# An attention and mixture-of-experts layer on 8 cores: the next window's layer norms cut into pieces between projections, and break points in TensorE's background work

## The chip, the cores and the metric

The kernel runs on the 8 cores of one Trainium2 chip. Each core takes 2048 of the 16384 tokens and works alone. The metric is the device time of the slowest core, in microseconds (us). Before the change it is 2968.38 us, the median of 3 runs (2964.4 to 2970.36).

The engines of a core are named as the profile names them: PE is TensorE (matmuls; PEld its weight loads), DVE is VectorE, ACT is ScalarE, POOL is GpSimd, SP is SyncE, which here only issues DMAs.

## The reference

What is computed, cut to what matters (LN is a layer norm without scale and shift):

```python
def layer(x):                                   # x: (2, 8192, 1024)
    h = LN(x)
    Q, K, V = h @ W_q + b_q, h @ W_k + b_k, h @ W_v + b_v
    Q, K, V = [(a).reshape(n, 16, l, 64) for a in (Q / 32, K / 32, V)]
    A = softmax(einsum('neax,nebx->neab', Q, K), axis=2)    # over a
    out = diagonal(A, axis1=2, axis2=3)[..., None] * V
    x = x + out.reshape(n, l, 1024) @ W_o + b_o
    f = LN(x)
    e = argmax(f @ Wr.T + br)                   # one of 8 experts for each token
    return x + W2[e] @ relu(W1[e] @ f + b1[e]) + b2[e]
```

The reshape makes 512 consecutive tokens of the program's input one head: within such a window of 512 tokens each token gives 16 queries and 16 keys of 64 elements, and only the diagonal of the softmax is used, so the kernel needs the sum of exp(score) for each of 8192 rows of a window and nothing else of the scores.

## The kernel before

**Windows.** A core has four windows (w = 0 to 3) of 512 tokens. For each it must compute the scores of 8192 by 8192, take their exponential and sum them. That is done in 64 rows of score tiles (r), each in five score groups of 3, 3, 4, 3, 3 (or 3, 3, 3, 4, 3) tiles of 128x512. PE writes a group into one half of PSUM (line 407), ACT takes exp over it with a running sum (line 520), and the two halves alternate: PE may write group n only when ACT is done with group n-2. So there are 320 score groups in a window and 1280 in all.

**Background work.** Everything else of the attention is cut into units by Python generators on PE's side and put between the score groups. After each group PE's budget `spare` grows by 1.5 or 2.5 units (at most 1.0 is carried over), and the loop takes units from the generator `fill` until the budget is used up. A unit is about one matmul of 128x512. What the units are:

- `proj` (line 253): 8 matmuls for 128 channels of Q, K or V over the window's 512 tokens. DVE then evacuates the tile with a bias (lines 591, 605 and 615).
- `swap_k` (line 264) and `diag` (line 272): after a tile of keys, the halves of its partitions swapped, and the diagonal scores, which serve as the exponent's offset. DVE makes what they read (605, 608) and takes what they give (596, 598).
- `xlt` (line 239): transposes of a normed tile of 128 tokens, which DVE copies to `XLT` (line 586).
- `tail`: when a quarter of a window (128 tokens, t = 0 to 3) has its sums, the reciprocal is turned (317), spread over the heads (326, twice), multiplied with V by DVE (645), projected with `W_o` (339), added to x (651), transposed (353), and put through the router (363, 374, 375). In between stand the pieces of the next window's Q, K, norms and of this window's V, as the table `PIECES[quarter][gap]` says: four quarters, in each four gaps in the tail.

**One bank.** During the attention all background work shares a single PSUM bank (`ONE_BANK`). A unit that takes the bank waits until DVE has evacuated the bank's last content, and DVE takes its instructions strictly in the order in which they are written. PE also takes its own in order, so while a background unit waits, the next score group waits behind it.

**Norms.** `norm(w, tc)` on DVE (line 578) makes one tile of 128 tokens: two `bn_stats`, one `bn_aggr`, ten steps on one column each (mean, variance, and three Newton steps for the inverse root), then the normed tile into one of two `XN` buffers. Two of the four norms of the next window stand together, `("n", 0), ("n", 1)`, in the first gap of quarter 0; the other two are in the first gap of quarter 1. For window 1 the first two follow the eight V tiles of window 0 directly.

**After the attention** the last quarter's tail runs alone, and then eight experts, in which PE runs matmuls of 320 columns nearly without a pause.

Of the kernel before, what the change touches and what calls it, by code (L numbers as in the profile page):

```python
# [9 lines left out]
F32 = mybir.dt.float32  # L10
# [6 lines left out]
P = 128  # L17
# [35 lines left out]


PIECES = (
# [11 lines left out]
def build_nc():  # L67
# [26 lines left out]
    with ExitStack() as st:  # L94
# [29 lines left out]
        NWU = S("NWU", [P, 1], F32); NWY = S("NWY", [P, 1], F32)  # L124
        NMN = S("NMN", [P, 1], F32)
        LG = S("LG", [P, 8], F32); LW = S("LW", [P, 8], F32)
        RMX = S("RMX", [P, 1], F32); RM2 = S("RM2", [P, 1], F32)
# [86 lines left out]
        def _(e):  # L214
# [16 lines left out]
            def pause(n):  # L231
                for _ in range(n):
                    yield 0

            def xlt(w, tc):
                b = bank()
                e.wait_ge(vXN, 4 * w + tc + 1)
                for c in range(DC):
                    mm = e.transpose(bf(b)[:, c * P:(c + 1) * P],
                                     XN[:, tc % 2, c * P:(c + 1) * P], IDB[:])  # L240
                    if c % 2 == 1 and c < DC - 1:
                        yield 1
                mm.then_inc(pM, 1)
                MARK["xlt", w, tc] = kM
                yield 1

            def proj(w, g, mc):
                if w == 0 and mc == 0:
                    e.wait_ge(sW[g], 16)
                b = bank()  # L250
                e.wait_ge(vM, MARK["xlt", w, 3])
                for kc in range(DC):
                    mm = e.matmul(PS[:, b, :], WR[:, g, kc, mc * P:(mc + 1) * P], XLT[:, kc, :],  # L253
                                  start=(kc == 0), stop=(kc == DC - 1))
                    if kc < DC - 1:
                        yield 1
                mm.then_inc(pM, 1)
                MARK["qkv"[g], w, mc] = kM
                yield 1

            def swap_k(w, c):
                b = bank()
                e.wait_ge(vM, MARK["k", w, c])
                e.matmul(PS[:, b, :], SWAP[:], KB[w % 2][:, c, :], start=True, stop=True).then_inc(pM, 1)
                MARK["s", w, c] = kM
                yield 1

            def diag(w, c):
                b = bank()
                e.wait_ge(vPR, DC * w + c + 1)  # L270
# [41 lines left out]
            def tail(w, t, pw, q):  # L312
# [7 lines left out]
                yield from pieces(pw, q, 0)  # L320
                for h in range(2):
                    b = bank()
                    if h == 0:
# [8 lines left out]
                if w + t == 0:  # L332
                    e.wait_ge(sW[3], 16)
                for hh in range(2):
                    b = bank()
                    if hh == 0:
# [9 lines left out]
                yield from pause(2)  # L346
                for hh in range(2):
                    b = bank()
                    if hh == 0:
# [36 lines left out]
            for w in range(NR):  # L386
# [7 lines left out]
                for r in range(64):  # L394
# [6 lines left out]
                    for size in SLOTS[r % 2]:  # L401
# [11 lines left out]
                        n += 1  # L413
                        spare = min(spare + SPARE[size], SPARE[size] + 1.0)
                        while spare > 0 and r >= hold:
                            cost = next(fill, 0)
                            if cost < 0:
                                hold = -cost
                            elif cost == 0:
                                break  # L420
                            else:
                                spare -= cost
                for _ in fill:
                    pass
# [123 lines left out]
        def _(e):  # L548
# [9 lines left out]
            def step(op):  # L558
# [4 lines left out]
                e.wait_ge(vS, nS)  # L563

            def stats(xt):

                for i in range(2):
                    step(e.bn_stats(BN6[:, i, :], xt[:, i * 512:(i + 1) * 512]))  # L568
                step(e.bn_aggr(MV[:], BN6[:].rearrange("p a b -> p (a b)")))
                step(e.tensor_scalar(NMN[:], MV[:, 0:1], -1.0, None, ALU.mult))  # L570
# [6 lines left out]

            def norm(w, tc):
                e.wait_ge(sXA[tc], 16 * (w + 1))
                stats(XA[:, tc, :])  # L580
                e.tensor_scalar(XN[:, tc % 2, :], XA[:, tc, :], NMN[:], NWY[:],
                                ALU.add, ALU.mult).then_inc(vXN, 1)
# [35 lines left out]
            def pieces(w, q, gap):  # L618
                for kind, i in PIECES[q][gap] if w < NR else ():
                    if kind == "v":  # L620
                        value(i)
                    elif w + 1 < NR:
                        if kind == "n":
                            norm(w + 1, i)
                        elif kind == "x":
# [70 lines left out]
            step(e.tensor_scalar(BKS[:], BKS[:], SCALE, None, ALU.mult))  # L696
            norm(0, 0)
            norm(0, 1)
            xlt(0)
            norm(0, 2)  # L700
            xlt(1)
            norm(0, 3)
            xlt(2)
# [11 lines left out]
            step(e.tensor_scalar(CN1[:], CN0[:], float(FIRST + 1), None, ALU.add))  # L715
            for c in range(DC):
                value(c)
            norm(1, 0)
            norm(1, 1)
            for w in range(NR):  # L720
# [306 lines left out]
```

## Time and profile before

| | |
|---|---|
| median of the runs | 2968.38 us |
| profiled execution | 2967.23 us |
| its span, first to last instruction, slowest core | 2965.5 us |
| spans of the eight cores | 2955.9 to 2965.5 us |
| PE busy | 2255.3 us, 76% |
| ACT busy | 2164.3 us, 73% |
| DVE busy | 539.5 us, 18% |
| chain that ended last | PE 41%, ACT 40%, issue 12%, DVE 5% |

The shares are means over two stages with different limits. In the attention ACT's exponentials fill most of the time; in the experts it is PE. "Granted clock" is the share of TensorE's full 2.4 GHz that the chip let through; 0.50 is its lower level of 1.2 GHz.

### The profile page before, as it was taken

The numbers are of one execution on the slowest core, as the hardware profiler recorded it, in microseconds if no ns is written. First come the engines' busy times: TensorE is split into PE (matmuls) and PEld (weight loads), VectorE is DVE, ScalarE is ACT, GpSimd is POOL, SyncE is SP. The second block draws the span as 40 slices with busy tenths as digits, with TensorE's granted clock in tenths as the row PEclk, the third lists the DMA queues.
The fourth block names the chain that finished last, engine by engine and source line by source line (L and its number), as shares of the span: only waits on it lengthen the run. The fifth ranks groups of instructions, "written<-read, shape, count | busy, mean of one in ns | idle before, by whom it ended". The sixth has DMA issues, their size and how long they took to land.

```text
span 2965.5 us, 31530 instructions; the slowest of 8 cores (2955.9 to 2965.5 us)
## 1 busy us (share of the span) xinstructions
PE 2255.3 (76%) x10592; PEld 840.3 (28%) x10592; DVE 539.5 (18%) x1309; ACT 2164.3 (73%) x2721; POOL 144.2 (5%) x201
## 2 busy tenths in 40 slices
PE   3876777867776878676767777776676599999997
PEld 1221111211121212111112121111111277777775
DVE  3113111121220112212111111110110212222221
ACT  0897999898989998898999889999999211111110
POOL 0000000000000000001000000000000001111100
PEclk9686675657675656675776657655555699999998
DMA  9999999999999999993000000030000278878773
GB/s 188 135 108 113 118 118 123 116 119 115 117 115 121 124 117 116 115 116 45 18 8 11 1 18 7 11 124 0 11 8 4 75 245 257 256 251 257 251 243 83
DMA packets 38163, 324.55 MB, mean 109 GB/s; under 512 B 8784, under 2 KB 9680, under 8 KB 25712
## 3 DMA queue, kind: packets, MB, share of 16 engines
q0 software_dynamic: 16224, 157.39, 45.7%
q1 hardware_dynamic: 21776, 165.05, 16.6%
q8 instruction: 95, 1.56, 0.2%
q14 instruction: 68, 0.56, 0.1%
HBM read 443.70 MB, written 159.73 MB: 203 GB/s over the span
## 4 chain that ended last, share of the span: by engine, by line
PE 41%; ACT 40%; issue 12%; DVE 5%; DMA 1%; DVEq 0%; SPq 0%; POOL 0%; ACTq 0%; POOLq 0%
ACT EA L520 20%; ACT EB L520 20%; PE PS L407 11%; PE PS L479 9%; PE PS L491 9%; PE PS L253 5%; PE PS L272 1%; PE PS L363 1%; PE PS L339 1%; DVE BN L568 1%; DVE AR L605 1%; PE PS L453 1%; DMA GM<-c_gm 1%; DVE AR L596 1%; PE PS L353 1%
## 5 line engine op out<-in xcount | busy, mean ns | idle before, releaser
L407 PE MATMUL PS<-AR 64*128 64x512 bf16 x4096 | 1124.4, 538 | 492.5 <-ACT EA L520 274.1
L520 ACT ACTIVATE EA<-PS,NEGD 128x1536 bf16<-128x1536 f32 (+1 forms) x640 | 1120.1, 1750 | 86.0 <-PE PS L407 83.8
L520 ACT ACTIVATE EB<-PS,NEGD 128x1536 bf16<-128x1536 f32 x640 | 1010.9, 1580 | 75.7 <-PE PS L407 75.0
L407 PEld LDWEIGHTS PS<-AR 64*128 64x128 bf16 x4096 | 172.9, 100 | 1221.2 <-issue 1218.1
L253 PE MATMUL PS<-XLT,WR 128*128 128x512 bf16 x768 | 307.6, 486 | 14.3 <-DVE VB L615 7.1
L532 ACT ACTIVATE AR<-PS,B1C 128x320 bf16<-128x320 f32 x128 | 67.5, 527 | 274.7 <-PE PS L479 274.7
L491 PE MATMUL PS<-AR,WR 128*128 128x320 bf16 x1664 | 229.9, 299 | 0.0
L479 PE MATMUL PS<-AR,WR 128*128 128x320 bf16 x1600 | 224.1, 301 | 1.0 <-DVE AR L742 1.0
L538 ACT ACTIVATE XR<-PS,B2C 128x320 f32<-128x320 f32 x32 | 16.9, 527 | 270.7 <-PE PS L491 270.7
L491 PEld LDWEIGHTS PS<-AR,WR 128*128 128x128 bf16 x1664 | 162.1, 98 | 62.0
L479 PEld LDWEIGHTS PS<-AR,WR 128*128 128x128 bf16 x1600 | 157.4, 98 | 62.5 <-issue 1.3
L520 ACT ACTIVATION_READ_ACCUMULATOR EB<-PS,NEGD 128x1 f32 x640 | 156.9, 245 | 0.0
L520 ACT ACTIVATION_READ_ACCUMULATOR EA<-PS,NEGD 128x1 f32 x640 | 156.3, 244 | 0.0
L253 PEld LDWEIGHTS PS<-XLT,WR 128*128 128x128 bf16 x768 | 61.2, 105 | 287.8 <-issue 279.0
L767 DVE TENSOR_SCALAR AR<-PS,B1C 128x320 bf16<-128x320 f32 x128 | 70.3, 549 | 196.2 <-PE PS L479 187.1
L635 DVE TENSOR_REDUCE ZS<-ZC 128x16 f32<-128x80 f32 x16 | 3.8, 235 | 547.4 <-ACT EB L520 547.4
L339 PE MATMUL PS<-WR,SA 128*128 128x512 bf16 x256 | 95.7, 459 | 1.7 <-DVE SA L645 1.1
L605 DVE TENSOR_SCALAR AR<-PS,BKS 128x512 bf16<-128x512 f32 x32 | 24.0, 751 | 243.1 <-PE PS L253 243.1
L363 PEld LDWEIGHTS PS<-WRT,X1T 128*128 128x128 f32 x256 | 53.4, 290 | 50.4 <-issue 50.4
L615 DVE TENSOR_SCALAR VB<-PS,BV 128x512 bf16<-128x512 f32 x32 | 24.0, 751 | 226.0 <-PE PS L253 226.0
L272 PE MATMUL PS<-GM,PROD 128*128 128x2 f32 x256 | 47.2, 306 | 23.4 <-DVE AR L596 22.5
L923 POOL DMA_DIRECT2D w1b<-w1t x64 | 31.5, 492 | 666.5 <-DMA w1b<-w1t 604.9
(93 smaller groups left out, 1093.8 us busy)
## 6 DMA issues: line engine op xcount, KB each, us to landing
w1b<-w1t POOLq DMA_DIRECT2D x64, 1024.0 KB, 19.4
w2b<-w2t POOLq DMA_DIRECT2D x64, 1024.0 KB
WR<-w2b SPq DMA_DIRECT2D x26, 2048.0 KB
WR<-w1b SPq DMA_DIRECT2D x25, 2048.0 KB
XA<-w1b SPq DMA_DIRECT2D x7, 2048.0 KB
XA<-w2b SPq DMA_DIRECT2D x6, 2048.0 KB
XA<-x SPq DMA_DIRECT2D x16, 512.0 KB, 53.4
XR<-x SPq DMA_DIRECT2D x16, 512.0 KB, 44.7
```

Source lines behind the costliest of these rows:

```text
L253: mm = e.matmul(PS[:, b, :], WR[:, g, kc, mc * P:(mc + 1) * P], XLT[:, kc, :], start=(kc == 0), stop=(kc == DC - 1))
L272: mm = e.matmul(PS[:, b, 2 * t0:2 * t0 + 2], PROD[:, c % 2, t0 * P:(t0 + 1) * P], GM2[:], start=True, stop=True)
L339: mm = e.matmul(PS[:, b, :], SA[:, kc, :], WR[:, 3, kc, hh * 512:(hh + 1) * 512], start=(kc == 0), stop=(kc == DC - 1))
L363: mm = e.matmul(PS[:, b, 0:8], X1T[:, c, :], WRT[:, c, :], start=(c == 0), stop=(c == DC - 1))
L407: mm = e.matmul(PS[:, (n % 2) * 4 + i, :], kb[w % 2][hp:hp + 64, gb // 2, t0 * P:(t0 + 1) * P], QB[w % 2][hp:hp + 64, ga // 2, :], start=T ...
L479: mm = e.matmul(PS[:, b, 0:cols], w1[:, kc, (k % 8) * P:(k % 8 + 1) * P], XGF[:, eg % 2, kc, 0:cols], start=(kc == 0), stop=(kc == DC - 1))
L491: mm = e.matmul(PS[:, b, 0:cols], w2[:, j, (dc % 2) * P:(dc % 2 + 1) * P], HB[:, j, 0:cols], start=(j == 0), stop=(j == NF - 1))
L520: e.activation(EO[n % 2][:, 0:size * 512], PS[:, b0:b0 + size, :].rearrange("p a b -> p (a b)"), AF.Exp, bias=NEGD[:, w % 2, t0, gb:gb + 1 ...
L532: e.activation(HB[:, k, 0:cols], PS[:, k % 4, 0:cols], AF.Relu, bias=B1C[:, ei * NF + k:ei * NF + k + 1]).then_inc(aCH, 1)
L605: e.tensor_scalar(KB[w % 2][:, c, :], PS[:, b, :], SCALE, BKS[:, c:c + 1], ALU.mult, ALU.add).then_inc(vM, 1)
L767: e.tensor_scalar(HB[:, k, 0:cols], PS[:, k % 4, 0:cols], B1C[:, ei * NF + k:ei * NF + k + 1], 0.0, ALU.add, ALU.max).then_inc(vCH, 1)
L923: e.dma_start(out=w1b[ei][i * 128:(i + 1) * 128, :], in_=w1t[ei][i * 128:(i + 1) * 128, :]).then_inc(sC1, 16)
```

## The change

Two things are changed, and a third goes with the first.

1. **Norms in pieces.** `norm` is split in three. `tile_moments` makes mean and variance of one tile (two `bn_stats`, one `bn_aggr`). `tile_scales` makes offset and inverse root for all four tiles at once, in 13 steps of four columns. `tile_norm` writes one normed tile. In the table `PIECES` these are kinds "s", "c" and "a". They have no work on PE. Those of quarter 0 each stand in front of the evacuation of a V projection, the last two between the transposes of quarter 1. The table's entry for the first gap of quarter 0 is now empty.
2. **Break points.** Each unit that takes the bank first yields `None` (`breath`), except the router's. The loop stops there, if it has already taken a unit behind this score group, and goes on behind the next one.
3. At the program's start and for window 1 the norms are written in the same new form.

```diff
 PIECES = (
-    ((("n", 0), ("n", 1)), (("v", 0), ("v", 1), ("v", 2)),
-     (("v", 3), ("v", 4), ("v", 5)), (("v", 6), ("v", 7))),
-    ((("x", 0), ("n", 2), ("x", 1), ("n", 3)), (("x", 2), ("x", 3)),
+    ((), (("s", 0), ("v", 0), ("s", 1), ("v", 1), ("s", 2), ("v", 2)),
+     (("s", 3), ("v", 3), ("c", 0), ("v", 4), ("a", 0), ("v", 5)), (("a", 1), ("v", 6), ("v", 7))),
+    ((("x", 0), ("a", 2), ("x", 1), ("a", 3)), (("x", 2), ("x", 3)),
...
+            def breath():
+
+                yield None
+
             def xlt(w, tc):
+                yield from breath()
                 b = bank()
...
             def proj(w, g, mc):
+                yield from breath()
...
             def swap_k(w, c):
+                yield from breath()
                 b = bank()
...
             def diag(w, c):
+                yield from breath()
                 b = bank()
...
                         spare = min(spare + SPARE[size], SPARE[size] + 1.0)
+                        begun = False
                         while spare > 0 and r >= hold:
                             cost = next(fill, 0)
-                            if cost < 0:
+                            if cost is None:
+                                if begun:
+                                    break
+                            elif cost < 0:
                                 hold = -cost
                             elif cost == 0:
                                 break
                             else:
                                 spare -= cost
+                                begun = True
...
+            def tile_moments(w, tc):
                 e.wait_ge(sXA[tc], 16 * (w + 1))
-                stats(XA[:, tc, :])
-                e.tensor_scalar(XN[:, tc % 2, :], XA[:, tc, :], NMN[:], NWY[:],
+                moments(XA[:, tc, :], MVX[:, tc, :])
+
+            def tile_scales():
+
+                step(e.tensor_scalar(NMX[:], MVX[:, :, 0], -1.0, None, ALU.mult))
+                step(e.tensor_scalar(NXH[:], MVX[:, :, 1], 0.5, 0.5 * EPS, ALU.mult, ALU.add))
+                step(e.tensor_scalar(NXI[:], NXH[:].bitcast(I32), 1, None, ALU.logical_shift_right))
+                step(e.tensor_scalar(NWX[:].bitcast(I32), NXI[:], -1.0, MAGIC, ALU.mult, ALU.add))
+                for _ in range(3):
+                    step(e.tensor_tensor(NXU[:], NWX[:], NWX[:], ALU.mult))
+                    step(e.tensor_tensor(NXU[:], NXU[:], NXH[:], ALU.mult))
+                    step(e.scalar_tensor_tensor(NWX[:], NXU[:], 1.5, NWX[:], ALU.subtract, ALU.mult))
+
+            def tile_norm(tc):
+                e.tensor_scalar(XN[:, tc % 2, :], XA[:, tc, :], NMX[:, tc:tc + 1], NWX[:, tc:tc + 1],
                                 ALU.add, ALU.mult).then_inc(vXN, 1)
...
-            norm(0, 0)
-            norm(0, 1)
+            for tc in range(4):
+                tile_moments(0, tc)
+            tile_scales()
+            tile_norm(0)
+            tile_norm(1)
             xlt(0)
-            norm(0, 2)
+            tile_norm(2)
             xlt(1)
-            norm(0, 3)
+            tile_norm(3)
             xlt(2)
             xlt(3)
...
             for c in range(DC):
+                if c < 4:
+                    tile_moments(1, c)
+                elif c == 4:
+                    tile_scales()
+                elif c < 7:
+                    tile_norm(c - 5)
                 value(c)
-            norm(1, 0)
-            norm(1, 1)
```

On DVE, at the start of window 1, before the change: the end of the second of two norms of `XA`, then the two products with V (`SA`), then three V tiles (`VB`).

```order
L575 SCALAR_TENSOR_TENSOR NWU<-NWY,NWH 128x1
L576 SCALAR_TENSOR_TENSOR NWY<-NWU,NWY 128x1
L581 TENSOR_SCALAR XN<-XA,NMN,NWY 128x1024
L645 TENSOR_TENSOR SA<-PS,VB 128x512 x2
L615 TENSOR_SCALAR VB<-PS,BV 128x512 x3
L651 TENSOR_TENSOR XR<-PS,XR 128x512 x2
```

The same place on DVE after the change, from the copy of the turned sums (`WRS`) on.

```order
L680 COPY WRS<-PS 16x128
L684 TENSOR_TENSOR SA<-PS,VB 128x512 x2
L586 BN_STATS BN<-XA 128x6 x2
L587 BN_AGGR MVX<-BN 128x2
L650 TENSOR_SCALAR VB<-PS,BV 128x512
L586 BN_STATS BN<-XA 128x6 x2
L587 BN_AGGR MVX<-BN 128x2
L650 TENSOR_SCALAR VB<-PS,BV 128x512
```

Between `WRS` and `SA` nothing is left; the moments of a tile stand ahead of each V tile.

On PE, in quarter 3 of window 0, before: score groups (L407) with the units between them. `KB` and `KS` are parts of `AR`; L264 is `swap_k`, L272 `diag`, L326 the spreading over heads.

```order
L407 MATMUL PS<-AR 128x512 x3
L253 MATMUL PS<-XLT,WR 128x512
L407 MATMUL PS<-AR 128x512 x3
L264 MATMUL PS<-AR,SWAP 128x512
L272 MATMUL PS<-GM,PROD 128x2 x4
L407 MATMUL PS<-AR 128x512 x10
L326 MATMUL PS<-WRS,GMB 128x128 x8
```

The same place after the change (L421 are the score groups).

```order
L421 MATMUL PS<-AR 128x512 x3
L262 MATMUL PS<-XLT,WR 128x512
L421 MATMUL PS<-AR 128x512 x3
L274 MATMUL PS<-AR,SWAP 128x512
L421 MATMUL PS<-AR 128x512 x3
L283 MATMUL PS<-GM,PROD 128x2 x4
L421 MATMUL PS<-AR 128x512 x7
L338 MATMUL PS<-WRS,GMB 128x128 x4
L421 MATMUL PS<-AR 128x512 x3
L338 MATMUL PS<-WRS,GMB 128x128 x4
```

A score group now stands between `swap_k` and `diag`, and one between the two halves of the spreading.

## Rows read from the trace of the kernel before

**Rows 1.** Busy time by stretch: attention, and all behind it

```profile
core 0: us, PE busy (x) PEld busy (x) DVE busy (x) ACT busy (x) POOL busy (x), PEclk, DMA share, GB/s
73.00:2314.00 2241.00, 1626.29 (x5943) 387.11 (x5943) 365.48 (x978) 2079.08 (x2561) 77.46 (x143) 0.64 0.60 75
2314.00:2965.00 651.00, 604.13 (x4531) 441.25 (x4531) 146.16 (x257) 84.33 (x160) 62.73 (x50) 0.96 0.68 218
```

**Rows 2.** Waits of ACT in the attention: total us, times, longest

```profile
ACT EA L520 <- PE PS L407: 83.8, 70, 8.9
ACT EB L520 <- PE PS L407: 75.0, 82, 12.0
```

**Rows 3.** ACT timeline (start, us): first group, score row 46 and next, last group

```profile
73.38 1.54 ACT L520 ACTIVATE EA<-PS,NEGD 128x1536 bf16<-128x1536 f32 x1
...
490.84 1.57 ACT L520 ACTIVATE EA<-PS,NEGD 128x1536 bf16<-128x1536 f32 x1
...
498.84 1.60 ACT L520 ACTIVATE EB<-PS,NEGD 128x1536 bf16<-128x1536 f32 x1
...
2312.04 1.67 ACT L520 ACTIVATE EB<-PS,NEGD 128x1536 bf16<-128x1536 f32 x1
```

**Rows 4.** ACT timeline: the groups behind norms, with the idle before them

```profile
243.79 1.54 ACT L520 ACTIVATE EB<-PS,NEGD 128x1536 bf16<-128x1536 f32 x1 [12.04 <-PE PS L407]
...
260.44 1.54 ACT L520 ACTIVATE EA<-PS,NEGD 128x1536 bf16<-128x1536 f32 x1 [5.03 <-PE PS L407]
...
674.68 1.97 ACT L520 ACTIVATE EA<-PS,NEGD 128x2048 bf16<-128x2048 f32 x1 [8.91 <-PE PS L407]
...
820.49 1.97 ACT L520 ACTIVATE EA<-PS,NEGD 128x2048 bf16<-128x2048 f32 x1 [6.81 <-PE PS L407]
```

**Rows 5.** Waits of PE in the attention, those on DVE: total us, times, longest

```profile
PE PS L326 <- DVE SA L645: 42.8, 15, 8.6
PE PS L272 <- DVE AR L596: 22.5, 24, 1.2
PE PS L264 <- DVE AR L605: 16.5, 20, 1.2
PE PS L317 <- DVE DGT L637: 12.7, 1, 12.7
```

**Rows 6.** Start of the program, timeline of POOL, DVE and PE

```profile
14.88 0.93 POOL L914 DMA_DIRECT2D WR<-wk  x1 [12.04 <-DMA XA<-x]
...
24.67 1.49 DVE L568 BATCH_NORM_STATS2 BN<-XA 128x6 f32<-128x512 f32 x2 [0.17 <-DVE BKS L696]
26.27 0.21 DVE L569 BATCH_NORM_AGGREGATE MV<-BN 128x2 f32<-128x12 f32 x1
...
29.43 0.81 DVE L581 TENSOR_SCALAR XN<-XA,NMN,NWY 128x1024 bf16<-128x1024 f32 x1
...
47.28 0.81 DVE L581 TENSOR_SCALAR XN<-XA,NMN,NWY 128x1024 bf16<-128x1024 f32 x1
...
50.19 17.45 PE L253 MATMUL PS<-XLT,WR 128*128 128x512 bf16 x72 [0.94 <-DVE XLT L586]
```

**Rows 7.** The DMA issue of the K weights, us to landing last

```profile
WR<-wk POOLq DMA_DIRECT2D x1, 2048.0 KB, 26.3
```

**Rows 8.** PE and ACT, joined units (window 0, quarter 3)

```profile
523.47 0.38 PE L264 MATMUL PS<-AR,SWAP 128*128 128x512 bf16 x1 [0.46 <-DVE AR L605]
...
524.89 1.84 PE L272 MATMUL PS<-GM,PROD 128*128 128x2 f32 x8 [1.05 <-DVE AR L596]
...
527.79 1.54 ACT L520 ACTIVATE EB<-PS,NEGD 128x1536 bf16<-128x1536 f32 x1 [2.48 <-PE PS L407]
```

**Rows 9.** PE and ACT, the same units with a score group between them

```profile
591.70 0.38 PE L264 MATMUL PS<-AR,SWAP 128*128 128x512 bf16 x1 [0.45 <-DVE AR L605]
...
593.12 1.02 PE L272 MATMUL PS<-GM,PROD 128*128 128x2 f32 x8 [0.35 <-DVE AR L596]
...
594.96 1.55 ACT L520 ACTIVATE EB<-PS,NEGD 128x1536 bf16<-128x1536 f32 x1
```

**Rows 10.** PE at its lower clock: units and score groups in turn

```profile
290.71 1.01 PE L253 MATMUL PS<-XLT,WR 128*128 128x512 bf16 x2
291.65 1.03 PE L407 MATMUL PS<-AR 64*128 64x512 bf16 x3
292.62 1.04 PE L253 MATMUL PS<-XLT,WR 128*128 128x512 bf16 x2
```

More of the change, by code:

```diff
@@ L125, in build_nc @@
         NMN = S("NMN", [P, 1], F32)
+        MVX = S("MVX", [P, 4, 2], F32); NMX = S("NMX", [P, 4], F32); NWX = S("NWX", [P, 4], F32)
+        NXH = S("NXH", [P, 4], F32); NXI = S("NXI", [P, 4], I32); NXU = S("NXU", [P, 4], F32)
         LG = S("LG", [P, 8], F32); LW = S("LW", [P, 8], F32)
@@ L321, in tail @@
                 for h in range(2):
+                    yield from breath()
                     b = bank()
@@ L334, in tail @@
                 for hh in range(2):
+                    yield from breath()
                     b = bank()
@@ L347, in tail @@
                 for hh in range(2):
+                    yield from breath()
                     b = bank()
@@ L563, in step, with moments, stats @@
                 e.wait_ge(vS, nS)
-            def stats(xt):
+            def moments(xt, mv):
                 for i in range(2):
                     step(e.bn_stats(BN6[:, i, :], xt[:, i * 512:(i + 1) * 512]))
-                step(e.bn_aggr(MV[:], BN6[:].rearrange("p a b -> p (a b)")))
+                step(e.bn_aggr(mv, BN6[:].rearrange("p a b -> p (a b)")))
+            def stats(xt):
+                moments(xt, MV[:])
                 step(e.tensor_scalar(NMN[:], MV[:, 0:1], -1.0, None, ALU.mult))
@@ L576, in stats @@
                     step(e.scalar_tensor_tensor(NWY[:], NWU[:], 1.5, NWY[:], ALU.subtract, ALU.mult))
-            def norm(w, tc):
+            def tile_moments(w, tc):
                 e.wait_ge(sXA[tc], 16 * (w + 1))
-                stats(XA[:, tc, :])
-                e.tensor_scalar(XN[:, tc % 2, :], XA[:, tc, :], NMN[:], NWY[:],
+                moments(XA[:, tc, :], MVX[:, tc, :])
[10 more added lines that the diff above has]
+                e.tensor_scalar(XN[:, tc % 2, :], XA[:, tc, :], NMX[:, tc:tc + 1], NWX[:, tc:tc + 1],
                                 ALU.add, ALU.mult).then_inc(vXN, 1)
@@ L622, in pieces @@
                     elif w + 1 < NR:
-                        if kind == "n":
-                            norm(w + 1, i)
+                        if kind == "s":
+                            tile_moments(w + 1, i)
+                        elif kind == "c":
+                            tile_scales()
+                        elif kind == "a":
+                            tile_norm(i)
                         elif kind == "x":
@@ L716, in _ @@
             for c in range(DC):
+                if c < 4:
+                    tile_moments(1, c)
+                elif c == 4:
+                    tile_scales()
+                elif c < 7:
+                    tile_norm(c - 5)
                 value(c)
-            norm(1, 0)
-            norm(1, 1)
             for w in range(NR):
```

## The prediction

> **What bounds the kernel now.** I read the busy time by stretch first. It splits the profiled execution at 2314 us: before it lies the attention, with ACT busy for 2079 of 2241 us; behind it the experts, with PE busy for 604 of 651 us at a granted clock of 0.96 [rows 1]. The change writes nothing behind 2314 us, so I take those 651 us as fixed, and ask what the attention's 2241 us and the 73 us ahead of it lose.
>
> In the attention the reader should look for how far ACT is from running back to back. One row of five score groups takes 498.84 - 490.84 = 8.00 us where nothing disturbs it; 256 of them make 2048 us. The attention lasts from 73.38 us to the end of the last group, 2312.04 + 1.52, which is 2240 us [rows 3]. So 192 us are lost. The waits of ACT show the same: 83.8 + 75.0 = 158.8 us in 152 waits, all on PE's score groups [rows 2]. (The view gives less than 192 because it leaves out the shortest gaps and because about 0.1 to 0.25 us of reading the accumulator, which otherwise overlaps, is exposed at each.) That is all that any change of the background work can win.
>
> Next, why PE was late. Its waits on DVE in this stretch are 42.8 + 22.5 + 16.5 + 12.7 = 94.5 us in the four largest rows, and about 117 us with a dozen small ones [rows 5]. PE runs in order, so a unit waiting for DVE holds the next score group back. The other 75 us or so of the 192 are PE's own work: bursts of units that are too long for one group's period at the lower clock. Two units and the next score group start 1.91 us apart (290.71 to 292.62) [rows 10], against the 1.52 us that ACT needs for three tiles.
>
> The change touches both kinds of DVE wait: the norms, and the short waits for the one bank.
>
> **The start.** Today four norms of some 5.5 to 6 us stand in a chain, each with its ten single steps, from 24.67 us to the first projection at 50.19 us [rows 6]. From the first norm: the two `bn_stats` with the aggregate take 26.27 - 24.67 + 0.31 = 1.91 us; from there to 29.43 us is 2.85 us for ten steps, 0.285 us a step. New chain: four moments 4 x 1.91 = 7.6 us; 13 steps 3.7 us (four columns instead of one; I give them the same price, since these times are hardly those of elements); then until the last norm starts, three norms of 0.73 us and two copies of 0.7 us, 3.6 us. That puts the last norm at 39.6 us, and from there to the first projection is 50.19 - 47.28 = 2.9 us as now: 42.5 us instead of 50.2. I take 7 us of the 7.7. The new form needs all four input tiles before the first norm; they are there, since POOL saw them by 14.88 us. Behind it are eight Q projections without a wait, 14 us at the 17.45 us for 72 matmuls, so K weights are wanted at 56 us; they were issued at 14.88 us and landed 26.3 us later, at 41 us [rows 6, 7]. Bounds: 4 us if the steps of four columns are twice as dear, 8 us else. **-7 us.**
>
> **The norms.** ACT stands 12.04 and 5.03 us behind the two pairs of norms in window 0, 8.91 and 6.81 us in window 1 [rows 4]; window 2 repeats window 1's with 8.92 and 7.00. The sum is 48.7 us; window 3 has no successor. What comes in their place: four moments of 1.9 us, one block of 13 steps of 3.7 us, and norms of 0.8 us, each in front of a V evacuation. What hides them is the V projection itself. It has 8 units and is spread over five or six score groups of 1.52 us, so DVE has about 7.5 us from one V tile to the next, and is busy for only 365 of 2241 us [rows 1]. The longest piece plus the evacuation, 3.7 + 0.75 us, fits. If that cover were gone the piece would hold back one evacuation, and PE would wait for the rest of it: 15 us of pieces a window, which is again the old loss. In quarter 1 a norm of 0.8 us remains between two transposes; that too falls under the score group which now follows. In window 0, the turning of the sums follows the last V unit with no break and waits for that evacuation and four short DVE steps, about 1 us beyond what is hidden. Bounds: 40 us (a fifth stays) to 50 us. **-48 us.**
>
> **The breaks.** Of the 117 us of PE's waits on DVE, about 49 are the norms', the 12.7 and the five long ones under the 42.8 [rows 5]. The other 68 are evacuations awaited by a unit that follows another one in the same gap. In the joined form swap and diagonal wait 0.46 and 1.05 us and ACT then idles 2.48 us [rows 8]. With a score group between them, which the old order happens to give at one place in each of windows 0 to 2, PE still waits 0.45 and 0.35 us, but those waits fall in time that PE has, and ACT's group at 594.96 us starts without idle [rows 9]. By the order of instructions there are 54 gaps of the joined kind before the change and 3 after it; groups with more than one bank unit behind them nearly vanish, while the number of score groups with any unit rises from 739 to 787.
>
> Not all 68 us come home. The diagonal's matmuls take 1.84 us at the lower clock against 1.02 at the higher [rows 8, 9]; with the next score group's 0.97 us that is 2.8 us in a period of 1.52, so even a lone diagonal costs about 0.9 us in perhaps 16 of its 30 places, 14 us. The break also leaves budget over, and up to 1.0 unit of it is spent at once later: openings with three projection matmuls rise from 30 to 46, and nine with four appear. A quarter of the saving could go that way, but the joined gaps that it replaces carried the same matmuls, so I book only 2 us. 68 - 14 - 2 = 52. Bounds: 20 us (only the longest joined gaps gain) to 68 us. **-52 us.** No unit is pushed out of its window: the last unit of windows 0 to 2 stands behind score group 304 of 320, before it was 303.
>
> **The sum.** 7 + 48 + 52 = 107 us. Against the profiled execution's own 2967.2 us (its span 2965.5 and 1.7 around it): 2860.2 us. The median of the runs shown lies 1.2 us above that execution, so 2861 us; the attention would lose 92 us to waiting instead of 192.
>
> **The clock.** Over the attention the granted clock is 0.64 on average, a mixture of the two levels 0.50 and 1.00 [rows 1]. The Trainium skill says against this change ("TensorE: Matmul & The Clock Gate", section "A second HAM failure mode: psum-queue depth-cycling") that short idle times between groups of matmuls make the clock swing between its two levels, and that what is lost is the time at the lower one; breaks make more and shorter pauses. By that rule the second rival below would come out. In this trace both levels occur beside such pauses already, so it bears the rule out only in part.
>
> **The rivals.**
>
> *Breaks only move the waits.* The bank is still one, and the budget left over comes back as longer bursts. Then the breaks win nothing and the norms and the start all: 2968.4 - 7 - 48 = 2913 us. For it: openings of three matmuls rise by half. Against it: the separated pair in rows 9 runs without idle.
>
> *The lower clock throughout, slower than before.* Place: the attention. If PE stayed at 0.50 in all of it, each gap would have its price at that level. The new order has 318 score groups with two units behind them, 1.91 - 1.52 = 0.39 us each, 124 us; 172 with three or more, at 0.47 a unit 0.83 us or so, 142 us; 297 with one unit give back 0.07 each (21 us), and 94 stretches without units give back one lead of about 0.42 (39 us). 124 + 142 - 21 - 39 = 206 us lost, more than the 192 of today, and where the leads are not won back 245. With the start's 7 us: 2968.4 - 7 + 14 = 2975, up to 3014; I take 2985 us. It decides from where the attention loses more than 199 us. Against it: DVE waits vanish, so PE stands still less.
>
> *Higher clock.* A mean of 0.64 from levels 0.50 and 1.00 means 72% of the attention at the lower level [rows 1]. If without the long waits it were 62%, a seventh of the 92 us of bursts (13 us) would go, and most of the lone diagonals' 14 us, which arise at the lower level alone: 2861 - 26 = 2835 us.
>
> *The pieces don't hide.* V evacuations held up by moments, half of the norms' loss comes back: 2885 us.
>
> **How the numbers follow.** Main case 2861 us: 0.68, own range 2843 to 2885. Breaks move the waits, 2913: 0.12. Lower clock, slower: 0.03. Higher clock, 2835: 0.10. Pieces not hidden, 2885: 0.07. The range of 8 in 10 reaches from 2833 to 2902 us: the lower end takes in most of the higher-clock case and the bounds 8, 50 and 68; the upper one reaches part-way to the first rival. What a measurement of this kernel can tell from no change is about 0.2%, 6 us. All cases but the lower clock are faster by more than that, and part of that case lands within it: faster 0.96, same 0.01, slower 0.03.
>
> **What would show it.** In the profile after: first exp at about 66 us; no ACT idle above 3 us in the attention; 256 rows in about 2140 us; PE's waits on DVE for the spreading over heads under 8 us instead of 42.8; `swap` and `diag` still waiting a few tenths each without ACT idle at the higher clock; the stretch behind the attention still 651 us. I am wrong in the breaks if ACT's waits stay above 110 us, in the norms if a gap of 5 us or more remains, and in the clock if the attention's mean is off 0.64 by 0.05 or more.

## The result, and the profile after

The kernel after takes 2844.61 us, the median of 4 runs (2841.02 to 2919.44), against 2967.62 us (2964.4 to 2970.36) for the kernel before on the same chip. The ratio is 0.9581, with a 95% interval of 0.9566 to 0.9596: 123 us or 4.2% faster. Forecast were 2861 us, within 2833 to 2902. The run of 2919.44 us is one in which part of the chip was disturbed; the ratios and the ranges of runs below leave such runs out and the medians don't, so where they disagree the ratio is to be read.

The profiled execution's span is 2839.3 us on its slowest core, 126.2 us less than before. First the busy time by stretch on core 0, which answers [rows 1]; the columns are the same.

```profile
67.00:2188.00 2121.00, 1569.21 (x5869) 378.06 (x5940) 350.28 (x896) 2072.73 (x2560) 78.17 (x143) 0.67 0.63 80
2188.00:2839.00 651.00, 603.76 (x4530) 441.44 (x4531) 146.18 (x257) 84.81 (x162) 62.74 (x50) 0.96 0.65 218
```

The stretch behind the attention is 651 us, as it was. The attention has gone from 2241 us to 2121 us with nearly the same ACT work, and its mean granted clock from 0.64 to 0.67 (0.65 to 0.67 as the mean of the eight cores). So all of the gain lies in two places, the start and ACT's idle time in the attention. This is the start on core 0 (start us, busy us, engine, line, operation), which answers [rows 6, 3]:

```profile
25.29 1.49 DVE L586 BATCH_NORM_STATS2 BN<-XA 128x6 f32<-128x512 f32 x2 [0.17 <-DVE BKS L735]
...
33.13 0.17 DVE L606 TENSOR_SCALAR NMX<-MVX 128x4 f32<-128x4 f32 x1
...
37.07 1.53 DVE L616 TENSOR_SCALAR XN<-XA,NMX,NWX 128x1024 bf16<-128x1024 f32 x2
...
43.99 2.29 PE L262 MATMUL PS<-XLT,WR 128*128 128x512 bf16 x5 [0.95 <-DVE XLT L621]
...
67.14 1.54 ACT L539 ACTIVATE EA<-PS,NEGD 128x1536 bf16<-128x1536 f32 x1
```

The first projection starts at 43.99 us instead of 50.19, and the first exponential at 67.14 instead of 73.38: 6.2 us less, although the chain of norms starts 0.62 us later than it did. The chain itself is therefore 6.8 us shorter.

The waits of ACT and of PE in the attention, on core 0 (who waits for whom: us in total, times, longest), which answer [rows 2, 5]:

```profile
ACT EB L539 <- PE PS L421: 24.4, 57, 2.1
ACT EA L539 <- PE PS L421: 20.5, 41, 2.5
```

```profile
PE PS L283 <- DVE AR L631: 4.4, 9, 1.1
PE PS L274 <- DVE AR L640: 2.4, 6, 0.6
PE PS L262 <- DVE VB L650: 2.3, 4, 0.7
PE PS L328 <- DVE DGT L676: 1.8, 1, 1.8
```

ACT waits 44.9 us instead of 158.8, and no wait is longer than 2.5 us where the longest was 12.04. PE's waits on DVE add up to 12.6 us instead of about 117. The spreading over heads (L338 now, L326 before), which carried the largest of them with 42.8 us, has no row at all.

For the comparisons below I use one measure of ACT's loss: the distance from the start of an exponential to the start of the next, less 1.515 us for three tiles or 1.94 us for four (4 x 1.515 + 1.94 = 8.00 us, the undisturbed row of [rows 3]). Summed over the attention it gives 192 us before and 73 us after on core 0, and 189.0 and 70.2 us as means of the eight cores. Sorted by what stands between the score groups, the means of the eight cores are:

| us lost by ACT | before | after |
|---|---|---|
| gaps with `swap_k` or `diag` | 56.4 | 11.6 |
| gaps with the spreading or the turning (the norms stood there) | 59.4 | 1.7 |
| other gaps with several users of the bank | 15.4 | 0 |
| gaps with one unit or with bursts of matmuls | 54.9 | 54.1 |

(Gaps without any unit hold the missing 3 us.) What is left after the change is nearly all PE's own work, and nearly all of it is lost at the lower clock: of the 70.2 us, 65 fall in places where the granted clock was 0.50 from the one exponential to the next, and 1.7 where it was 1.00. Before, it was 161 and 9.6 us of 189.0.

At the place of the old gap of 8.91 us [rows 4], window 1 on core 0 now reads:

```profile
616.04 1.68 ACT L539 ACTIVATE EB<-PS,NEGD 128x1536 bf16<-128x1536 f32 x1
616.43 1.04 PE L421 MATMUL PS<-AR 64*128 64x512 bf16 x4
617.40 0.60 PE L338 MATMUL PS<-WRS,GMB 16*128 16x128 bf16 x4
617.57 2.10 ACT L539 ACTIVATE EA<-PS,NEGD 128x2048 bf16<-128x2048 f32 x1
618.72 1.48 DVE L586 BATCH_NORM_STATS2 BN<-XA 128x6 f32<-128x512 f32 x2
619.43 1.06 PE L262 MATMUL PS<-XLT,WR 128*128 128x512 bf16 x2 [0.47 <-issue]
619.53 1.66 ACT L539 ACTIVATE EB<-PS,NEGD 128x1536 bf16<-128x1536 f32 x1
```

The two halves of the spreading (L338) have a score group between them, and ACT runs back to back. The batch statistics begin at 618.72 us, where nothing on PE waits for DVE. (The 0.47 us ahead of the projection's row is a matmul that is missing from the records; its weight load stands in the trace at 619.02 us.)

And the swap and the diagonal at the place where [rows 8] had them joined:

```profile
487.92 0.39 PE L274 MATMUL PS<-AR,SWAP 128*128 128x512 bf16 x1
488.66 1.55 ACT L539 ACTIVATE EA<-PS,NEGD 128x1536 bf16<-128x1536 f32 x1
488.92 0.59 PE L421 MATMUL PS<-AR 64*128 64x512 bf16 x3 [0.61 <-ACT EB L539]
489.44 1.05 PE L283 MATMUL PS<-GM,PROD 128*128 128x2 f32 x8
490.17 1.55 ACT L539 ACTIVATE EB<-PS,NEGD 128x1536 bf16<-128x1536 f32 x1
491.69 1.99 ACT L539 ACTIVATE EA<-PS,NEGD 128x2048 bf16<-128x2048 f32 x1
```

ACT's idle time of 2.48 us has gone entirely. Two things differ here, not one: the diagonal also took 1.05 us, the price of the higher clock, where it took 1.84 us before.

### The profile page after: what moved, and what is told of

Its sections match the earlier page's. It is cut to its first block, busy times and chain, and to the rows that moved or that the text cites. A ratio compares the mean times of both kernels' runs of the same rounds, so it can differ in the third digit from the quotient of the medians.

```text
span 2839.3 us, 31237 instructions; the slowest of 8 cores (2830.4 to 2839.3 us)
## 1 busy us (share of the span) xinstructions
PE 2197.8 (77%) x10515; PEld 831.5 (29%) x10592; DVE 519.6 (18%) x1201; ACT 2158.7 (76%) x2721; POOL 144.9 (5%) x201
## 4 chain that ended last, share of the span: by engine, by line
ACT 47%; PE 37%; issue 13%; DVE 1%; DMA 1%; SPq 0%; POOL 0%; DVEq 0%; ACTq 0%; POOLq 0%
ACT EA L539 24%; ACT EB L539 23%; PE PS L498 10%; PE PS L510 10%; PE PS L421 9%; PE PS L262 4%; PE PS L377 1%; PE PS L283 1%; PE PS L472 1%; DMA GM<-c_gm 1%; PE PS L352 0%; PE PS L458 0%; DVE BN L586 0%; DMA out_t<-VB,PAD 0%; PE PS L367 0%
## 5 line engine op out<-in xcount | busy, mean ns | idle before, releaser
L421 PE MATMUL PS<-AR 64*128 64x512 bf16 x4096 | 1107.3, 526 | 518.1 <-ACT EA L539 291.2
L421 PEld LDWEIGHTS PS<-AR 64*128 64x128 bf16 x4096 | 171.7, 99 | 1213.9 <-issue 1211.7
L262 PE MATMUL PS<-XLT,WR 128*128 128x512 bf16 x707 | 282.2, 482 | 18.8 <-issue 11.0
L352 PE MATMUL PS<-WR,SA 128*128 128x512 bf16 x240 | 85.6, 435 | 4.8 <-issue 2.5
L498 PE MATMUL PS<-AR,XA 128*128 128x320 bf16 x448 | 62.8, 299 | 0.0
L973 POOL DMA_DIRECT2D w2b<-w2t x64 | 31.5, 492 | 598.4 <-DMA w2b<-w2t 598.4
```

Source lines behind the costliest of these rows:

```text
L352: mm = e.matmul(PS[:, b, :], SA[:, kc, :], WR[:, 3, kc, hh * 512:(hh + 1) * 512], start=(kc == 0), stop=(kc == DC - 1))
L421: mm = e.matmul(PS[:, (n % 2) * 4 + i, :], kb[w % 2][hp:hp + 64, gb // 2, t0 * P:(t0 + 1) * P], QB[w % 2][hp:hp + 64, ga // 2, :], start=T ...
L498: mm = e.matmul(PS[:, b, 0:cols], w1[:, kc, (k % 8) * P:(k % 8 + 1) * P], XGF[:, eg % 2, kc, 0:cols], start=(kc == 0), stop=(kc == DC - 1))
L973: e.dma_start(out=w2b[ei][i * 128:(i + 1) * 128, :], in_=w2t[ei][i * 128:(i + 1) * 128, :]).then_inc(sC2, 16)
```

## The experiments

Unless something else is said, the edit is shown against the kernel after (- is a line taken out, + one put in), and the loss is ACT's by the measure above, the mean of eight cores. Ratios are to the kernel before, with their 95% intervals.

**Norms only.** The norms' new form, with the break points silent, so that PE's order is that of before.

```diff
 def breath():
+    return
     yield None
```

> The norms in pieces (start included), no break points: TensorE's order is that of the kernel before. Theory A (the two parts add up, each removes its own waits on VectorE): the six gaps of 5 to 12 us vanish and the start gains 6 us, so 2967 - 49 - 6 = about 2912 us; ScalarE's waits in the attention stay near 110 us. Theory B (the pieces need the breaks, because without a score group between units a moment in front of a V evacuation is waited for): less than half of the 49 comes, 2935 us or more. Theory C (the breaks do nothing but move waits): 2845 to 2855 us, as the full change.

Measured: ratio 0.9857 [0.9747, 0.9967], runs 2922.8 to 2936.3 us, and a loss of 149.0 us: 40.0 less than before. The joined gaps are as they were. On core 1 PE still waits at the diagonal and the swap, as much as in [rows 5]:

```profile
PE PS L284 <- DVE AR L632: 24.2, 27, 1.2
PE PS L275 <- DVE AR L641: 15.1, 18, 1.2
PE PS L339 <- DVE SA L685: 14.2, 15, 0.9
```

The spreading (L339) has kept 15 waits of at most 0.9 us; the long ones behind norms are gone. At the norms' own places the loss fell by 41.9 us. By these waits the pieces hide; the 17.5 us that stay in these gaps are those of the spreadings and turnings themselves, which still stand joined. The six gaps behind norms alone lost 49.9 us before and lose 7.7 now, so only 42.2 us of them were the norms'. That is theory A's mechanism, but not its number: the runs lie 11 to 24 us above its 2912 us.

**Breaks only.** The old norms, at the start too, with the break points active.

```diff
-((), (("s", 0), ("v", 0), ("s", 1), ...
+((("n", 0), ("n", 1)), (("v", 0), ("v", 1), ("v", 2)), ...
-((("x", 0), ("a", 2), ("x", 1), ("a", 3)), ...
+((("x", 0), ("n", 2), ("x", 1), ("n", 3)), ...
```

> The break points alone, norms whole and in their old places, start as before; TensorE's order is that of the full change. Theory A (the parts add up): the full change gained about 125 us, of which start 6 and norms 49, so the breaks are worth 70 us: 2897 us; the six gaps of 5 to 12 us are still there. My prediction's size for the breaks, 52 us, would give 2915 us. Theory C (breaks only move waits): within 6 us of 2967 us.

Measured: ratio 0.9755 [0.9672, 0.9838], runs 2896.2 to 2909.8 us, a loss of 120.9 us: 68.1 less than before. PE's waits on DVE on core 2:

```profile
PE PS L338 <- DVE SA L686: 28.5, 5, 7.6
PE PS L328 <- DVE DGT L678: 12.7, 1, 12.7
...
PE PS L274 <- DVE AR L646: 3.6, 7, 0.6
PE PS L283 <- DVE AR L637: 3.5, 7, 1.0
```

Swap and diagonal together wait 7.1 us instead of 39.0. Of the long waits only the norms' remain, six of up to 12.7 us. So the breaks do not move the waits to another place. In bursts they do give some back: ACT loses 75.5 us less in the first three kinds of gap of the table, and 7.9 us more in gaps with one unit or bursts (62.8 against 54.9). The two parts alone give 40.0 + 68.1 = 108.1 us, and together 118.8.

**The start only.**

```diff
 # the table, norm() and window 1 as in the kernel before
 def breath():
+    return
     yield None
```

> Only the first window's norms at the program's start in the new form; all else as before. Theory A: the first exponential comes 6 to 7 us earlier and the end follows one for one, 2961 us (ratio 0.998). Rival: the start is hidden behind weights or constants that land later, 2967 us.

Measured: 2960.58 us, ratio 0.9971 [0.9943, 0.9998], about 7 us less (by the interval, just told apart from no change), with an attention that loses as much as before (187.4 us). The waits of ACT over the whole span, on the slowest core; the third is the one ahead of the first score group, and the other two are nearly those of [rows 2]:

```profile
ACT EA L540 <- PE PS L422: 83.6, 63, 9.3
ACT EB L540 <- PE PS L422: 75.6, 81, 12.4
ACT L540 <- PE PS L422: 66.0, 1, 66.0
```

The start is worth what the sum gave it.

**Breaks at swap and diagonal only.** The new norms; the other units (`xlt`, `proj`, the tail's) take the bank without a break.

```diff
 def proj(w, g, mc):
-    yield from breath()
...  # the same in xlt and at three places of tail
```

> Norms in pieces, and breaks only in front of the key swap and the diagonal; projections, transposes, head spreading and output projection follow each other without a break. In the trace before, gaps with swap and diagonal joined to something else carried about 47 of the 74 us that ScalarE idled behind joined units. Theory A1 (each joined gap pays for itself): 47 of the breaks' 70 us are kept, 2912 - 47 = 2865 us. Theory A2 (what counts is that no unit waits for the bank anywhere): well above that, 2885 us. Theory A3 (the other breaks cost more in longer bursts than they save): 2845 us or less.

Measured: ratio 0.9685 [0.958, 0.9789], median 2880.1 us, a loss of 105.2 us. The gaps with swap or diagonal fell from 55.2 us (norms only) to 17.1, while the spreading's 15.6 and the other joined gaps' 16.0 are near norms only's 17.5 and 15.1. On core 1 PE's waits on DVE are again, in the first place, those of the units that were left joined:

```profile
PE PS L335 <- DVE SA L679: 14.2, 15, 0.9
PE PS L260 <- DVE VB L645: 8.9, 9, 1.1
PE PS L362 <- DVE X1T L689: 5.7, 6, 0.9
```

Swap (L272) and diagonal (L281) wait 4.2 and 3.9 us here. The time is nearer to the 2885 us of theory A2, but only because theory A1 counted from 2912 us: norms only came out at 2926 us (the middle one of its runs), and 47 us less is 2879. So A1 holds: each kind of joined gap pays for itself, and parting one hardly touches the others.

**Moments and scales in one block.** What the pieces would cost if nothing covered them: all four moments and the scales in the first gap of quarter 0, as the norms stood.

```diff
-((), (("s", 0), ("v", 0), ("s", 1), ("v", 1), ("s", 2), ("v", 2)),
- (("s", 3), ("v", 3), ("c", 0), ("v", 4), ("a", 0), ("v", 5)), ...
+((("s", 0), ("s", 1), ("s", 2), ("s", 3), ("c", 0)), (("v", 0), ("v", 1), ("v", 2)),
+ (("v", 3), ("v", 4), ("a", 0), ("v", 5)), ...
```

> The full change, but in windows 1 and 2 the moments of all four tiles and the scales stand as one block in the first gap of quarter 0, behind the turned sums, where no projection covers them; the two norms of single tiles stay in front of V tiles. TensorE's order is that of the full change. It tests whether it is the place in front of a projection that hides the work. Theory A (only the cover counts): the block is 4 x 1.9 + 3.7 = 11.3 us; of the two old norms' 11 us in that place ScalarE idled 8.9 us, so some 9 us come back in each of two windows, 18 us, 2863 us; ScalarE shows two gaps of about 9 us. Theory B (a long wait also sends TensorE to its lower clock, and the bursts behind it cost more): 25 us or more, of which 7 or more lie outside the two gaps. Theory C (shorter work is enough, since four tiles share one set of scale steps): 5 us or less.

Measured: 2865.32 us, ratio 0.9654 [0.9639, 0.9669], 21 us slower than the kernel after, with a loss of 91.3 us. Here is DVE on core 6 in window 1, and the exponential that waited:

```profile
614.99 1.47 DVE L586 BATCH_NORM_STATS2 BN<-XA 128x6 f32<-128x512 f32 x2
...
622.80 0.17 DVE L606 TENSOR_SCALAR NMX<-MVX 128x4 f32<-128x4 f32 x1
...
626.04 0.16 DVE L613 SCALAR_TENSOR_TENSOR NWX<-NXU,NWX 128x4 f32<-128x4 f32 x1
```

```profile
628.85 1.54 ACT L539 ACTIVATE EB<-PS,NEGD 128x1536 bf16<-128x1536 f32 x1 [7.42 <-PE PS L421]
```

Four moments take 622.80 - 614.99 = 7.8 us and the 13 steps 3.4 us, against 7.6 and 3.7 in the prediction. The same work costs nothing in pieces and 7.4 us in a block. That makes 15.2 us in the two windows that have it. The other 6.0 us appeared in gaps with one unit or bursts, 3.7 of them in the first 80 groups of windows 1 and 2, behind the blocks: from score group 9 to 80 of window 1 the granted clock was 0.73 (mean of eight cores) where the kernel after has 0.78. So the result lies between theories A and B.

**Half the budget carried over.** An opening is a place where a projection begins; this removes most openings with three or four matmuls in one gap (55 before the edit, 12 with it).

```diff
-spare = min(spare + SPARE[size], SPARE[size] + 1.0)
+spare = min(spare + SPARE[size], SPARE[size] + 0.5)
```

> The full change with at most 0.5 instead of 1.0 unit of budget carried over. Openings with three or four projection matmuls fall from 55 to 12, the last unit of a window stands behind score group 307 instead of 304. In the trace after the change ScalarE idled 24 us behind those openings, of 73 us in all. Theory A (a burst costs because it is longer than one group's period and the lead; two units cost 0.39 us only where no lead is left): half of it goes, 2844 - 12 = 2832 us. Theory B (the same matmuls must be done somewhere, the idle only moves to the groups with two units): within 4 us of 2844 us.

Measured: 2840.25 us, ratio 0.9584 [0.9556, 0.9611], a loss of 69.0 us: no difference. ACT's waits (core 6) have only changed their shape, to more and shorter ones:

```profile
ACT EA L539 <- PE PS L421: 22.0, 63, 1.5
ACT EB L539 <- PE PS L421: 11.2, 35, 1.2
```

The matmuls of the long openings, spread out, cost the same elsewhere: gaps with three or four projection matmuls lose 18.3 us less, and those with two 16.7 us more.

**The diagonal in two halves, and more breaks.**

```diff
 # diag, after two of its matmuls
+if t0 == 1:
+    yield 2.5
...
-yield 2
+yield 1
 # and breath() ahead of router_sums, the router's logits and the turning
```

> The full change, with the diagonal's four matmuls cut into two pairs with a score group between them at most places, and break points also ahead of the router's units and of the turning of the sums. Theory A (the lone diagonal, 1.84 us at the lower clock, is still too long for a period; my prediction put 14 us on it, the trace after shows 6): 5 us of 11 us go, with 3 us more at the added breaks: 2844 - 8 = 2836 us. Theory B (no bank unit waits that could still be parted; longer background work only pushes bursts together): within 4 us of 2844 us.

Measured: 2847.88 us, ratio 0.9596 [0.9583, 0.9609], a loss of 74.1 us: nothing gained, possibly 4 us lost. ACT's waits on core 1:

```profile
ACT EB L544 <- PE PS L426: 27.5, 74, 0.8
ACT EA L544 <- PE PS L426: 22.0, 50, 2.4
```

The diagonal's long turn was not a cost worth removing.

**An extra score matmul.** The first matmul of a score group is issued twice where no unit preceded it, 489 times by the weight loads in the trace; the second overwrites the first with the same values.

```diff
-spare, hold = 0.0, 0
+spare, hold, begun = 0.0, 0, True
...
+if i == 0 and not begun:
+    mm = e.matmul(PS[:, (n % 2) * 4 + i, :], ...)   # once more
```

> The full change; in each score group that follows a group behind which no unit was taken (492 of them) the first tile's matmul is done twice, the second writing the same values. It adds work where TensorE is least busy, to see what the granted clock does. Theory A (the remaining 54 us of idle behind bursts come from the lower clock, and more activity raises it): the attention's granted clock goes from 0.66 to 0.75 or more, the idle falls by 10 to 25 us, 2820 to 2835 us. Theory B (the clock stays and the added 0.34 us a group fits into the period): 2844 us within 4. Theory C (the added work takes the lead that the next burst needs): 2850 us or more.

Measured: 2918.47 us, ratio 0.9833 [0.9819, 0.9846], 74 us slower than the kernel after, 0.15 us for each of the 489. The attention's row on core 7:

```profile
67.00:2187.00 2120.00, 1746.97 (x6245) 437.65 (x6243) 350.42 (x896) 2026.83 (x2469) 77.75 (x143) 0.66 0.63 80
```

By the records PE is busy for 1746.97 - 1569.21 = 178 us more in these 2120 us than in the kernel after, and the granted clock was 0.66 where that has 0.67. More work on PE did not bring it up. And a gap without background work is no free time: of the 76 us that ACT loses more (146.4 against 70.2), 63 lie in these very gaps. 453 of them were at the lower clock, where a matmul in a row of them takes 0.34 us [rows 10] and the added one cost 0.14 us; in the 24 at the higher clock it cost nothing. The other 13 us were lost elsewhere, which is what theory C spoke of: the lead that the next burst needs.

**A thinner order.** Less budget for each group, so that the units spread more evenly: first 1.25 and 2.25 with half a unit carried over, then 1.2 and 2.0. The third run is the kernel after again, for comparison on the same chip.

```diff
-SPARE = {3: 1.5, 4: 2.5}
+SPARE = {3: 1.25, 4: 2.25}      # the second: {3: 1.2, 4: 2.0}
...
+spare = min(spare + SPARE[size], SPARE[size] + 0.5)
```

> The full change with a smaller budget of background work behind each score group: 1.25 and 2.25 units instead of 1.5 and 2.5, at most 0.5 carried. The same units stand in 919 instead of 787 places, and places with more than two units fall from 172 to 83; the last unit of windows 0 to 2 stands behind group 313 of 320. Theory A (the remaining 70 us of idle are bursts longer than a period, so spreading them thinner helps): 12 to 20 us less than the full change, 2828 us. Theory B (as when only the carry was cut: the idle moves to places with two units, and the lead between bursts is what sets it): within 5 us of the full change, 2844 us. Theory C (thinner work lowers the granted clock): 2850 us or more.

> As the one before, with 1.2 and 2.0 units: 923 places with units, 51 with more than two, 327 with two. Theory A: 15 to 25 us less than the full change, 2824 us. Theory B: 2844 us within 5. Theory C: 2850 us or more, and a lower granted clock in the attention than 0.67.

> The changed kernel once more, on the same chip and in the same rounds as the two thinner orders, so that the three can be compared. All theories: 2844 us within 5.

Measured:

| | ratio, 95% | runs, us | loss, us |
|---|---|---|---|
| thin | 0.9543 [0.9511, 0.9574] | 2834.4 to 2838.5 | 63.6 |
| thinner | 0.9534 [0.9488, 0.9581] | 2832.7 to 2834.2 | 62.2 |
| after, again | 0.9581 [0.9543, 0.9619] | 2839.7 to 2850.1 | 71.2 |

The attention in the thinner order (core 1) and in the kernel after again (core 6):

```profile
67.00:2187.00 2120.00, 1656.81 (x5956) 390.34 (x5956) 353.22 (x903) 2072.82 (x2560) 77.67 (x143) 0.65 0.63 80
```

```profile
67.00:2187.00 2120.00, 1590.59 (x5939) 380.91 (x5939) 350.29 (x896) 2072.13 (x2559) 77.75 (x143) 0.67 0.63 80
```

The thinner order loses 9 us less although its clock is 0.65 and not 0.67, and PE is busy for 66 us more in it. A better clock is not what makes the difference between these orders. Gaps with one unit or bursts lose 17 us less (37.9 against 54.9), and those with swap, diagonal, spreading or turning 9 us more (22.4 against 13.7). It is the best version that was run: all its runs lie below all of the kernel after, by 13 us (0.5%) from middle to middle. The intervals of the ratios overlap, so the size of that gain is not settled. Theory A's direction is right; its 15 to 25 us are not quite reached.

## Why the prediction was right, and which term was mis-sized

**What bounds the kernel.** Right: all the gain came from ACT's idle time and the start, and the 651 us behind the attention stayed 651.

**The start, -7.** Measured -6.2 us in the profile, and about -7 us with the start alone. Right, and so was its working: 7.8 us for the moments (25.29 to 33.13) and 3.9 for the steps (to 37.07) against 7.6 and 3.7. The first projection came at 43.99 us and not at 42.5; 0.6 of these 1.5 us are the later start of the chain.

**The norms, -48.** The mechanism was right: the pieces hide behind the V projection, and uncovered they cost 7.4 us a window. Alone they gave 40.0 us, the lower bound. The 48.7 us that I read behind the norms were not all theirs: 7.7 us of those six gaps stayed with norms only, since the spreading and the turning still stood joined there, and went only with the breaks. Added to the breaks the pieces gave 120.9 - 70.2 = 50.7 us, of which 41.1 at their own places.

**The breaks, -52.** This is the term that was mis-sized. Alone the breaks gave 68.1 us, which was my bound and not my value, and the deduction of 14 us for diagonals that stand alone was the step that failed. I had priced 16 of 30 such places at the lower clock with 0.9 us. In the kernel after there are 29, and they lose 7.6 us (mean of eight cores): 12.5 of them lie wholly at the lower clock and lose 0.57 us each, the others 0.4 us in all. And 11 diagonals stood alone before already and lost 9.3 us, so nothing was to be deducted for the rest.

The term's other two numbers were off too, but against each other. I had read a joined gap's cost as PE's wait on DVE alone, 68 us (it was 71, since the norms' waits were 12.7 + 33.4 = 46 us and not 49); with the breaks alone all gaps with swap, diagonal, spreading, turning or several users of the bank lost 75.5 us less. And for budget left over I had booked 2 us, where the gaps with one unit or bursts lost 7.9 us more. Only together with the norms' pieces did these gaps lose nothing more (54.9 and 54.1). Openings of three matmuls cost 46 x 0.35 us and those of four 9 x 0.60, 21.5 us together, against 30 x 0.63 = 18.8 before, and shortening them gave nothing back.

**The sum.** It left the attention a loss of 92 us; 73 us are left on core 0. Against the 100 us of the two terms the eight cores gained 118.8: 8.0 less from the norms alone, 16.1 more from the breaks alone, and 10.7 more because the two together give more than their sum. Errors of opposite sign thus brought the forecast nearer than its terms were. The last 10.7 us are not explained. They lie in gaps with one unit or bursts: the pieces alone made these lose 3.4 us more and the breaks alone 7.9, and both together 0.8 less; in every other kind of gap the two parts add up within 1 us. The clock goes with it in part. Behind the norms' place in window 1, from group 9 to 80, it is 0.78 after, 0.74 with breaks only and 0.73 with the block, so in the new order a long wait is followed by a lower clock. But before has 0.76 there, with the long wait, and norms only 0.75, without it. Why the old order differs stays open.

**The rivals.** That the breaks only move the waits (2913 us) fell with the breaks-only run: swap and diagonal waited 7.1 us and not 39.0. That the pieces don't hide (2885 us) fell too; with the block, where they can't, the time was 2865 us. The lower clock throughout, and slower, did not come: the mean rose to 0.67. And the breaks did not make more and shorter pauses, as I had argued: in the attention of core 0 PE waited 922 times before, for 0.66 us on average, and 898 times after, for 0.59 us, so the pauses became shorter but not more. The rule of the Trainium skill cited in the prediction ("TensorE: Matmul & The Clock Gate", section "A second HAM failure mode: psum-queue depth-cycling") spoke for such a loss. This case's traces agree with it in that the clock swings between its two levels all through the attention, before and after; with the breaks the attention is shorter and not longer, and since the pauses did not become more, a loss from more of them is not tested here. The higher clock (2835 us) came in part: the share of the lower level fell from 72% to 66% of the attention, where that rival took 62%. By its own arithmetic six tenths of its 26 us would make 2845 us, which is what was measured. That this is the cause is not shown, and the places speak against it: the gaps with one unit or bursts, where half of the 26 us should have come from, lose what they lost before, and the thinner order is faster still at 0.65.

**What was to be seen.** First exponential at about 66 us: 67.14. No idle above 3 us: 2.5 at most. 256 rows in 2140 us: 2121. PE's waits for the spreading under 8 us: none. Swap and diagonal still waiting a few tenths: fewer than forecast, 15 waits between them.

## What to carry to other kernels

When an in-order engine fills the gaps of the engine that bounds the kernel, put a piece of the main work between any two fillers that share one buffer: the wait for the buffer's evacuation then falls in time the engine has. Cut long work on the evacuating engine to less than the distance between two evacuations, and put each piece ahead of one that nobody awaits yet. To size such a change, add up the bounding engine's idle time place by place (start to start, less the undisturbed period), and not the waits of the filler engine: here the joined places and the norms' gave 117.9 of the 118.8 us that were won.

## What the runs showed that I had not expected

- A gap without background work has less room than it seems: 489 extra matmuls in such gaps cost 0.15 us each of the kernel's time, though ACT bounds it there. At the higher clock, where 24 of them stood, they cost nothing.
- Bursts cost next to nothing at the higher clock: of the 70.2 us that are left, 1.7 were lost there, in a third of all gaps.
- More work on PE did not raise the granted clock (178 us more of it: 0.66 against 0.67), and the order with the smallest loss had 0.65.
- Steps of four columns cost about what those of one do: from start to start 0.28 us for the TENSOR_SCALAR steps against 0.26, and 13 steps in 3.4 us against ten in 2.85.
- The same float32 matmuls of two columns, eight in the records, take 1.05 us at the higher clock and 1.84 at the lower.
